# An attention and expert layer on one core: the front end reordered around the first slot's row scores

## What is computed

```python
x = queries                                   # (8, 512, 128)
n = layernorm(x)
q, k, v = relu(n @ Wq.T + bq), relu(keys @ Wk.T + bk), relu(values @ Wv.T + bv)
a = softmax(qh @ kh.T / sqrt(8)) @ vh         # 16 heads of 8; keys and values are shared by the 8 batches
x = x + layernorm(merge(a) + n)
y = layernorm(x)                              # then an encoder layer over (128, 16, 128)
y1 = ln(y + mha(y, 4 heads)); y2 = ln(y1 + moe(y1))   # 8 experts, FF 512: (t @ w1 + b1) @ w2 + b2
out = x + layernorm(y2)
```

## Time and profile before

| | |
|---|---|
| median of 3 runs | 689.4 us (689.3 to 690.68) |
| profiled execution, its own time | 692.12 us |
| its span | 690.1 us |
| busy over the span | PE 528.1, DVE 543.7, ACT 422.0, POOL 229.0 us |
| mean granted TensorE clock | 0.895 |

### The profile page before, as it was taken

One profiled execution on the slowest core, in us unless ns is written; L12 is line 12 of the kernel. 1 busy time (PEld: TensorE's weight loads), 2 busy tenths in 40 slices (PEclk: granted clock), 3 DMA queues, 4 the chain that ended last, 5 costly groups with the idle time before them and its releaser, 6 DMA issues.

```text
span 690.1 us, 9879 instructions
## 1 busy us (share of the span) xinstructions
PE 528.1 (77%) x3439; PEld 209.3 (30%) x3439; DVE 543.7 (79%) x899; ACT 422.0 (61%) x882; POOL 229.0 (33%) x360
## 2 busy tenths in 40 slices
PE   1874898898988989989899888577477765998620
PEld 1650112222222222222222213465356643443300
DVE  4969678888989999899998950488965555799996
ACT  2650568878878788787887887333345223474653
POOL 6001000000031560315603173085044600766861
PEclk9995579999999999999999999869878697999955
DMA  9732011101221012210122000200000000000102
GB/s 246 237 131 103 13 30 28 36 22 32 61 65 36 22 33 61 65 34 23 34 62 63 20 9 17 61 2 0 1 1 1 1 1 0 0 2 0 30 23 69
DMA packets 31285, 28.92 MB, mean 42 GB/s; under 512 B 6132, under 2 KB 23676, under 8 KB 31236
## 3 DMA queue, kind: packets, MB, share of 16 engines
q1 hardware_dynamic: 29204, 27.31, 13.4%
q10 hardware_dynamic: 2032, 0.98, 0.5%
HBM read 19.23 MB, written 8.65 MB: 40 GB/s over the span
## 4 chain that ended last, share of the span: by engine, by line
PE 43%; DVE 34%; ACT 13%; POOL 5%; issue 3%; DMA 2%; ACTq 0%; DVEq 0%; SPq 0%
PE ps L1246 15%; DVE row_max L1417 14%; PE ps L1241 8%; ACT space L1352 6%; PE ps L1224 5%; PE ps L592 3%; DVE space L871 2%; DVE st L241 2%; PE ps L508 2%; DVE SC L754 2%; DVE space L751 2%; PE ps L577 1%; DVE space L862 1%; DMA w_in<-in_L_ffn_out_proj_w 1%; DVE space L264 1%
## 5 line engine op out<-in xcount | busy, mean ns | idle before, releaser
L1417 DVE TENSOR_REDUCE row_max<-ps 128x2 f32<-128x1024 f32 x256 | 300.5, 1219 | 38.3 <-PE ps L1224 38.2
L1352 ACT ACTIVATE space<-ps 128x512 f32<-128x512 f32 x512 | 264.2, 604 | 66.6 <-PE ps L1241 66.6
L1241 PE MATMUL ps<-space 51*128 51x512 bf16 x512 | 148.9, 391 | 34.1 <-ACT space L1352 33.4
L1246 PE MATMUL ps<-space 128*32 128x512 f32 x1024 | 139.9, 619 | 0.1
L1224 PE MATMUL ps<-space 48*128 48x512 bf16 x512 | 104.4, 403 | 11.8 <-DVE row_max L1417 10.1
L1119 POOL CAST max_parts<-row_max 128x16 bf16<-128x16 f32 x32 | 6.3, 196 | 291.4 <-DVE row_max L1417 291.4
L1241 PEld LDWEIGHTS ps<-space 51*128 51x128 bf16 x512 | 36.8, 95 | 119.3 <-ACT space L1352 103.3
L592 PE MATMUL ps<-W,space 128*128 128x512 f32 x128 | 70.6, 634 | 0.0
L1224 PEld LDWEIGHTS ps<-space 48*128 48x128 bf16 x512 | 25.1, 94 | 139.2 <-issue 77.3
L428 POOL TENSOR_TENSOR space<-PC,same_row 128x512 f32<-128x512 f32 x32 | 32.9, 1058 | 63.0 <-DVE PC L767 63.0
L709 ACT ACTIVATE space<-ps,weight 128x128 f32<-128x128 f32 x128 | 34.3, 383 | 20.8 <-PE ps L592 9.3
(11 more groups left out here) (192 smaller groups left out, 689.6 us busy)
## 6 DMA issues: line engine op xcount, KB each, us to landing
q_parts_dram<-space SPq DMA_DIRECT2D x2, 1536.0 KB, 5.4
space<-q_parts_dram SPq DMA_DIRECT2D x64, 48.0 KB
attended_dram<-attended SPq DMA_DIRECT2D x128, 18.0 KB
X<-in_L_attn_queries SPq DMA_DIRECT2D x8, 256.0 KB, 7.6
space<-in_L_ffn_w SPq DMA_DIRECT2D x2, 1024.0 KB, 5.9
space<-q_parts_dram SPq DMA_DIRECT2D x64, 32.0 KB
space<-attended_dram SPq DMA_DIRECT2D x16, 128.0 KB, 2.4
space<-inverses_dram SPq DMA_DIRECT2D x16, 128.0 KB
```

Of the source, the lines that this page charges most:

```text
L1241: pe.matmul(ps[:, col_bank(u), :], k_rows[rows_a, kappa // 4 % 2, tc * P:(tc + 1) * P], q_stack[rows_a, kappa % 4, b * S:(b + 1) * S], sta ...
L1246: mm = pe.matmul(ps[32 * m:32 * m + 32, PV, :], v_heads[:, tc, PAIR * (kappa // 4) + m % PAIR, :], probs[:, tc % 2, m, :], start=(tc == 0) ...
L1352: act.activation(probs[:, tc % 2, m, :], ps[:, col_bank(u), :], ACT.Exp, scale=1.0 / math.sqrt(DH)).then_inc(s_pr, 1)
L1417: dve.tensor_reduce(row_max[:, par].rearrange("p (a c) -> p a c", a=PAIR)[:, :, item], ring(n), AX.X, MAX).then_inc(s_free, 1)
```

## The change

Batches 4 to 7 are no longer turned by units but batch by batch (`turn_batch`) into banks 6 and 7 (`q_bank`), so that banks 0 to 3 are free as the ring. On TensorE fold 0 is followed by batch 4's transposes, the first two row scores of slot 0, and then rounds of a projection, the next batch's transposes and two row scores; then `turn_max` for slot 0, fold 1, and the rows of slot 1. ScalarE takes `root(act, 2)` behind the last evacuation of batch 3, `root(act, 3)` in fold 0 behind the copy of expert 2, and batches 4 to 7 between the folds. VectorE splits batches 0 to 3 ahead of norms 2 and 3, then sets the values, makes slot 0's eight reductions, split 4, `copy_turned` for slot 0, splits 5 to 7, `c_row`, and slot 1's reductions. SP loads shift 0 behind stack 1 and ahead of `store_q(1)`.

```diff
--- before.py
+++ after.py
@@ -282,13 +282,15 @@
             act.wait_ge(s_var, k + 1)
             act.activation(small[:, 2, :], small[:, 2, :], ACT.Sqrt).then_inc(s_sd, 1)
 
+        q_bank = lambda b: b if b < QB else 6 + b % 2
+
         def project_q(act, b):
 
             act.wait_ge(s_qp, b + 1)
             if b >= QB:
                 act.wait_ge(s_qs, b - QB + 1)
-            act.activation(qf[b % QB], ps[:, b % QB, :], ACT.Relu, bias=bias_col[:, 0:1])
-            act.activation(q_parts[:, 0, b * S:(b + 1) * S], ps[:, b % QB, :], ACT.Relu,
+            act.activation(qf[b % QB], ps[:, q_bank(b), :], ACT.Relu, bias=bias_col[:, 0:1])
+            act.activation(q_parts[:, 0, b * S:(b + 1) * S], ps[:, q_bank(b), :], ACT.Relu,
                            bias=bias_col[:, 0:1]).then_inc(s_qe, 1)
 
         W1T_BANK, W_BANK, C_BANK = 6, 5, 4
@@ -340,7 +342,7 @@
                 if e >= 2:
                     act.wait_ge(s_wu, e - 1)
                 act.copy(w1T[:, e % 2], ps[:, W1T_BANK + e % 2, :]).then_inc(s_w1c, 1)
-                if e == 5:
+                if e == 2:
                     root(act, 3)
 
         def copy_folded(act, r):
@@ -1042,6 +1044,8 @@
             sp.wait_ge(s_qst[0], 16)
             load_stack(0)
             load_stack(1)
+            sp.wait_ge(s_free, 9)
+            load_shift(0)
             store_q(1)
             sp.wait_ge(s_qst[1], 16)
             load_stack(2)
@@ -1049,9 +1053,6 @@
             c_rows = c_stack[0:PARTS, :].rearrange("q (r j d) -> q r j d", r=2, d=D)
             for j in range(E2):
                 sp.dma_start(c_rows[:, :, j, :], c_parts[32 * j:32 * j + 1]).then_inc(s_cl, 16)
-            sp.wait_ge(s_free, 8 + 3)
-            load_shift(0)
-
             def slot(kappa):
 
                 if kappa + 3 < NQ:
@@ -1193,27 +1194,30 @@
 
                 pe.wait_ge(s_xn, u + 1)
                 for g, b in UNITS[u]:
-                    mm = pe.transpose(ps[:, b % QB, g * P:(g + 1) * P], XN[:, g, b, :], ident[:])
+                    mm = pe.transpose(ps[:, b, g * P:(g + 1) * P], XN[:, g, b, :], ident[:])
                 mm.then_inc(s_xt, 1)
 
-            def project_half(half):
-                for b in range(QB * half, QB * half + QB):
-                    pe.wait_ge(s_xtc, b + 1)
-                    pe.matmul(ps[:, b % QB, :], wT[:, 0, :], featT[:, b, :], start=True, stop=True).then_inc(s_qp, 1)
+            def turn_batch(b):
+                pe.wait_ge(s_xn, 4)
+                if b >= QB + 2:
+                    pe.wait_ge(s_qe, b - 1)
+                for g in range(G):
+                    mm = pe.transpose(ps[:, q_bank(b), g * P:(g + 1) * P], XN[:, g, b, :], ident[:])
+                mm.then_inc(s_xt, 1)
+
+            def project_batch(b):
+                pe.wait_ge(s_xtc, b + 1)
+                pe.matmul(ps[:, q_bank(b), :], wT[:, 0, :], featT[:, b, :], start=True, stop=True).then_inc(s_qp, 1)
 
             turn_unit(0)
             turn_unit(1)
-            project_half(0)
+            for b in range(QB):
+                project_batch(b)
             pe.wait_ge(s_kpe, 1)
             pe.wait_ge(s_vpe, 1)
             pe.wait_ge(s_b1, 16)
             turn_b1(pe)
             fold_weights(pe, 0)
-            pe.wait_ge(s_qe, QB)
-            turn_unit(2)
-            fold_weights(pe, 1)
-            turn_unit(3)
-            project_half(1)
 
             def score_rows(n, kappa, item, waits):
 
@@ -1248,20 +1252,27 @@
                 if tc == TC - 1:
                     mm.then_inc(s_pv, 1)
 
+            pe.wait_ge(s_Wc, 1)
+            turn_batch(QB)
             pe.wait_ge(s_kl[0], 32)
             pe.wait_ge(s_ql[0], 96)
+            pe.wait_ge(s_qe, QB)
+            score_rows(0, 0, 0, None)
+            score_rows(1, 0, 1, None)
+            for b in range(QB, B):
+                project_batch(b)
+                if b + 1 < B:
+                    turn_batch(b + 1)
+                    for item in (2 * (b - QB) + 2, 2 * (b - QB) + 3):
+                        score_rows(item, 0, item, item - 1)
+            turn_max(8, 0, 7, 1)
             pe.wait_ge(s_qe, B)
-            n = 0
-            for item in range(8):
-                score_rows(n, 0, item, n - 1 if n >= 2 else None)
-                n += 1
+            fold_weights(pe, 1)
             pe.wait_ge(s_ql[1], 96)
+            n = 9
             for item in range(8):
                 score_rows(n, 1, item, n - 1)
                 n += 1
-                if item == 1:
-                    turn_max(n, 0, n - 1, 1)
-                    n += 1
             assert n == 17
             pe.wait_ge(s_shift, 32)
             pe.wait_ge(s_Wc, 2)
@@ -1326,23 +1337,25 @@
             act.wait_ge(s_kp, 1)
             act.activation(k_rest[:, 0], ps[:, 4, :], ACT.Relu, bias=bias_col[:, 1:2]).then_inc(s_kpe, 1)
 
-            def project_half(half):
-                act.wait_ge(s_xt, 2 * (half + 1))
-                for b in range(QB * half, QB * half + QB):
-                    act.copy(featT[:, b], ps[:, b % QB, :]).then_inc(s_xtc, 1)
-                    if b % QB in (1, 2):
-                        project_q(act, b - 1)
-                if half == 0:
-                    root(act, 2)
-                for b in range(QB * half + QB - 2, QB * half + QB):
-                    project_q(act, b)
-
-            project_half(0)
+            def copy_batch(b):
+                act.wait_ge(s_xt, 2 if b < QB else b - 1)
+                act.copy(featT[:, b], ps[:, q_bank(b), :]).then_inc(s_xtc, 1)
+
+            for b in range(QB):
+                copy_batch(b)
+                if b:
+                    project_q(act, b - 1)
+            project_q(act, QB - 1)
+            root(act, 2)
             copy_weights(act, 0)
             copy_folded(act, 0)
+            copy_batch(QB)
+            for b in range(QB, B):
+                if b + 1 < B:
+                    copy_batch(b + 1)
+                project_q(act, b)
             copy_weights(act, 1)
             copy_folded(act, 1)
-            project_half(1)
             act.wait_ge(s_bin, 16 * 3)
 
             def exps(kappa, tc):
@@ -1390,28 +1403,26 @@
             dve.wait_ge(s_bc, 16)
             dve.tensor_tensor(v_tmp[:], ps[:, 5, :].rearrange("p (c f) -> p c f", c=TC),
                               bv_row[:].rearrange("p (o f) -> p o f", o=1).broadcast_to([P, TC, D]), ADD).then_inc(s_vpe, 1)
+
+            def split_q(b):
+                cols = slice(b * S, (b + 1) * S)
+                dve.wait_ge(s_qe, b + 1)
+                ch.done(dve.tensor_tensor(rest[:, b % 2], qf[b % QB], q_parts[:, 0, cols], SUB))
+                ch.wait()
+                ch.done(dve.tensor_copy(q_parts[:, 1, cols], rest[:, b % 2]))
+                ch.wait()
+                dve.tensor_tensor(q_parts[:, 2, cols], rest[:, b % 2], q_parts[:, 1, cols], SUB).then_inc(s_qs, 1)
+
+            for b in range(QB):
+                split_q(b)
+            norm_unit(2)
+            norm_unit(3)
             dve.wait_ge(s_vpe, 1)
             dve.wait_ge(s_vset, 2)
             for c in range(TC):
                 dve.tensor_scalar(v_heads[:, c, :, 0:DH], v_tmp[:, c, :].rearrange("p (h d) -> p h d", d=DH),
                                   0.0, None, MAX).then_inc(s_vb, 1)
 
-            def split_q(b):
-                cols = slice(b * S, (b + 1) * S)
-                dve.wait_ge(s_qe, b + 1)
-                ch.done(dve.tensor_tensor(rest[:, b % 2], qf[b % QB], q_parts[:, 0, cols], SUB))
-                ch.wait()
-                ch.done(dve.tensor_copy(q_parts[:, 1, cols], rest[:, b % 2]))
-                ch.wait()
-                dve.tensor_tensor(q_parts[:, 2, cols], rest[:, b % 2], q_parts[:, 1, cols], SUB).then_inc(s_qs, 1)
-
-            norm_unit(2)
-            for b in range(QB):
-                split_q(b)
-            norm_unit(3)
-            for b in range(QB, B):
-                split_q(b)
-
             def reduce_rows(n, par, item):
                 dve.wait_ge(s_full, n + 1)
                 dve.tensor_reduce(row_max[:, par].rearrange("p (a c) -> p a c", a=PAIR)[:, :, item], ring(n), AX.X,
@@ -1422,20 +1433,18 @@
                 src = ps[0:PARTS * QB * TC, 2 * (n % 2), 0:P // 2].bitcast(BF16)
                 dve.tensor_copy(max_turned[:, par, :], src).then_inc(s_free, 1)
 
-            n = 0
             for item in range(8):
-                reduce_rows(n, 0, item)
-                n += 1
+                reduce_rows(item, 0, item)
+            split_q(QB)
+            copy_turned(8, 0)
+            for b in range(QB + 1, B):
+                split_q(b)
             dve.wait_ge(s_bw, 2)
             dve.wait_ge(s_b2, 16 * E2)
             dve.tensor_tensor(c_row[:], ps[:, C_BANK, P:3 * P].rearrange("p (r d) -> p r d", d=D), b2_sb[:],
                               ADD).then_inc(s_csum, 1)
             for item in range(8):
-                reduce_rows(n, 1, item)
-                n += 1
-                if item == 1:
```

(17 more changed lines are left out.)

## The result

The changed kernel takes 695.8 us in the median of 7 runs (694.24 to 700.91); the kernel before took 689.92 beside it. The ratio is 1.0093, with a 95% interval of 1.0061 to 1.0124: slower, outside the forecast range and on the other side of zero. The medians take in all runs, while the ratios and intervals leave out every run more than 1.5% above the fastest of its kernel, so a ratio need not be the quotient of the two medians. The profiled execution is the median one, 695.8 us with a span of 693.7, 3.6 more than before. That is less than the 5.9 us between the medians, because the profiled execution of the kernel before (692.12) lies 2.2 above that kernel's median.

What follows compares the result with a forecast made beforehand. No engine was full; the front end's chain of waits set the first exponential. First stack at 44.9 plus 26.4 put its table load at 71.3 instead of 73.27, 1.9 us gained: median 687.5, range 684.0 to 691.8.

Steps and rivals of the forecast that it cites:

- T: Time at which the first stack has landed and the first slot's scores can begin: 44.9 us, bounds 44.4 and 45.6.
- last of eight reductions, T +: First slot's eight reductions, bound by VectorE: 9.14 us, with the first score pair ending at T + 9.5.
- maxima to second fold: POOL splits the maxima in 1.1 us, TensorE turns them, and the second fold begins at T + 10.9.
- second fold and its wait: TensorE's second fold takes 7.04 us, to T + 18.0; VectorE, done at T + 16.9, waits 1.1 us.
- The store: SP issues the first half's store at 33.2, a gain of 2.6 us; the first stack load follows 5.5 us later.
- a rival at 0.12: Loads: the store meets the constant loads and T slips 1.5 us, or the third stack sets the pace; no change, 688.6 to 690.4.
- The rounds: Per two reductions (2.28 us) TensorE's scores, projection and transposes take 2.2 us at the high clock, 4.4 at the low.
- the slack: First fold and batch 4's transposes end at 42.8, 2.1 us ahead of T, so a low clock starting there costs nothing.
- the first rival: TensorE's clock stays low through the first fold, scores begin at about 47.7: 690.3 to 696, slower, chance 0.16.
- The roots on ScalarE: ScalarE waits in root(2) and root(3) ahead of first-fold copies; 7.3 us of stall, free while T sets the pace.
- SP's order: load_shift(0) ahead of store_q(1) delays nothing; the third stack lands at 73.0, asked for at 73.3, fitting by 0.3.
- The slots: TensorE's clock falls to 0.50 again at the first slot for about the same length, near 21 us; 0.38 us lost per us.

Runs made afterwards that it cites:

- Late constants: Changed kernel with SP's ten constant loads moved from ahead of store_q(0) to behind the second stack: 697.31 us, 1.0087 against the kernel before.
- norm 2 first: Changed kernel with the third norm again ahead of splits 0 to 3, root(2) back in its old place, root(3) behind the first fold: 696.29 us.
- Busy gap: Changed kernel with five more fp32 matmuls into an unread bank behind batch 4's transposes: 695.18 us, 1.0069 against the kernel before.
- Copy first: Changed kernel with VectorE's copy of the turned maxima ahead of split 4 instead of behind it: 694.21 us, 1.0037 against the kernel before.
- late constants with a busy end: Changed kernel with constant loads behind the second stack and repeated, unread score matmuls in the last two slots: 689.42 us, 0.9976 against the kernel before.
- fold early: Changed kernel with the second fold moved right behind the first, ahead of batch 4's transposes: 697.59 us, 1.0094 against the kernel before.
- three mends: Changed kernel with constant loads behind the second stack, two score pairs ahead of the second fold, repeated score matmuls in the last two slots: 692.16 us.

## Why the prediction was wrong, step by step

The sum asked for a table load at 71.3; it came at 79.72, 8.4 us later. The four terms that were off add up to just that, and in the other execution of this front end (77.24) the same four were off by 1.6, 2.0, 1.1 and 1.2:

| term | forecast | measured | off |
|---|---|---|---|
| first stack, T | 44.9 | 47.17 | 2.3 |
| last of eight reductions, T + | 9.5 | 12.45 | 2.9 |
| maxima to second fold | 1.4 | 2.5 | 1.1 |
| second fold and its wait | 7.1 | 9.2 | 2.1 |

**The store.** "Store to first stack load was 41.36 − 35.82 = 5.5 us" is the step that failed. I moved that 5.5 with the issue, and gave the constant loads 0.2 us in T, 0.9 by its upper bound, and 1.5 in a rival at 0.12. It took 7.75 (33.21 to 40.96), with bytes flowing at full rate only from 36.5. The gain of 2.6 us in issue was worth 0.4. Late constants and norm 2 first show it from both sides: with the constants behind the store, or nearly gone before it, the wait is 5.5 again.

**The rounds.** "It fits by 0.1 at the high level. At the low one it is 4.4 against 2.28" was right, and so was the rival's mechanism, but not its place. I had the low level in the first fold; there it came and went inside the slack (the fold ended at 41.5, 42.3 forecast). The stretch that mattered was the second one, 42.1 to 47.2, which my own sum contained as "2.1 us ahead of T" and which I booked as harmless cover. Busy gap took it away and shortened the way from first score to table load by 1.5 to 3.3 us. The holes between the reductions (1.47, 0.69 and 0.20 us) cost 2.9 us and not the 6.5 of three low rounds, because the clock came back in the second round. That the measured 695.8 lies inside the first rival's 690.3 to 696 is luck: its late first fold did not happen. And one argument against that rival was weak: the slow transposes at 12.68 are no sure sign of a low level, since the granted clock of 12.68 to 14.40 reads 1.00.

**The maxima.** I took POOL's 1.1 us from a trace in which VectorE reduced beside it; here it splits, and POOL took 2.1 us. Copy first shows the cause.

**The second fold.** Its 7.04 us were measured at the high clock. In the changed kernel more than half of it ran at 0.50 (until 67.1 of 62.1 to 71.3). TensorE had been idle for 3.2 us ahead of the turn.

**The roots on ScalarE.** "7.3 us of stall cost nothing while T sets the pace" holds for the changed kernel: the stand in root(2) was 5.33 us, and the fold and batch 4's transposes were still over 5 us before the first stack. With the store mended it no longer holds in full, since the first fold's end sets the first score. In late constants with a busy end:

```profile
36.22 1.12 PE L311 MATMUL ps<-ident,space 128*128 128x128 f32 x4 [6.07 <-ACT b1T L338]
...
44.10 1.08 PE L330 MATMUL ps<-space,b1T 128*32 128x128 f32 x32
...
45.70 0.61 PE L1228 MATMUL ps<-space 48*128 48x512 bf16 x4
```

By the 6.2 us from first stack load to first score in the changed kernel, the stack there would have allowed scores at 38.77 + 6.2 = 45.0, an estimate; so the roots then cost some 0.7 us.

**SP's order.** The third stack's loads went out at 73.87, in the place reckoned behind the splits, and the first slot did not wait for it. That rival had no part here, but the fit was as tight as reckoned: in copy first and fold early TensorE waited 0.1 and 0.6 us for the third stack.

**The slots.** I expected "about the same length" of the low stretch. It was 8 us instead of 20.9 and paid back 4.5 us. The kernel before, in another execution, had it end at 81.7 instead of 94.2, so this is not owed to the change. What ends such a stretch, and why three mends lost its start again, stays open; the runs show the size of the effect and not its cause.

Weighed up: in the profiled pair 6.45 us were lost at the table load, 4.5 came back up to the third turn, 1.6 went behind it, where the clock rose and fell at other points too and which I did not take apart. Over the runs with the slots' end kept busy, the loss is 3.1 us. The rest of the 5.9 us between the first medians is not taken apart.

## What to carry to other kernels

A DMA issued earlier lands earlier only if what was issued ahead of it has left the engines: here 2.6 us in issue became 0.4. Look at when its bytes begin to flow, not at when it was issued. An idle stretch ahead of dense TensorE work is not free cover: behind 5 idle us the first rounds ran at a granted clock of 0.50, so reckon the work behind it at both levels. Where the clock can fall in several places, pin those places in both kernels with work that nobody reads before judging a change of a few us; it took away the runs near 700 in two kernels here, though not in the changed one. And count an event in a trace from a point ahead of the edits, because the first transposes, the same in all kernels here, started up to 3 us apart.

## What the runs showed of the hardware

- Small POOL instructions took 0.59, 0.39 and 0.65 us beside VectorE's splits, and 0.20, 0.21 and 0.20 when VectorE stood or reduced from PSUM.
- Ten constant loads, most of their bytes in rows of 512, kept a 1.5 MB store from starting for 3.3 us behind its issue, moving 62 GB/s meanwhile, while the store itself then ran at some 350 to 430.
- In the slots' last 26.5 us TensorE's clock either held at 1.00 or fell to 0.50, at 131 matmuls against 94. The runs of the kernel before at 699 to 700 us have a mean granted clock of 0.88, those at 688 to 692 one of 0.90. With two more matmuls per step there, no run of the kernel before nor of late constants was above 694.1, but three of the changed kernel were at 698.6 to 700.5.
